# The first FFN half's router placed inside the last attention rows of an AdaLN attention and LoRA-MoE kernel, with a gate folded into the value weight

## What is computed

```python
mod = (silu(c) @ wmod)            # sa, ca, ga, sb, cb, gb for each batch; |ga|, |gb| at least 0.25
h = layernorm(x) * (1 + ca) + sa
x = x + ga * attn(h)              # attn: layernorm*gamma+beta, q k v, causal softmax, @ o_proj, + h
h = layernorm(x) * (1 + cb) + sb
x = x + gb * ffn(h)
# ffn:
gate_base, up_base = h @ Wg.T, h @ Wu.T
out = silu(gate_base) * up_base @ Wd.T
probs = softmax(h @ Wr.T); top-2 of 8 -> we for each expert
for each expert: hh = silu(gate_base + h@Ag.T@Bg.T*2) * (up_base + h@Au.T@Bu.T*2)
                 out += (hh @ Ad.T @ Bd.T * 2) * we
```

## Time and profile before

| | |
|---|---|
| time, median of 3 runs | 710.68 us (710.49 to 711.01) |
| profiled execution | 710.4 us, its span 708.6 us |
| granted TensorE clock, mean over the span | 0.992 |
| one batch | 165.9 us |
| PE busy | 665.5 us (94%), 3760 matmuls |
| PEld busy | 561.0 us (79%) |
| DVE busy | 509.1 us (72%), 1152 instructions |
| ACT busy | 340.2 us (48%), 604 |
| POOL busy | 392.2 us (55%), 518 |
| chain of work that ended last | PE 55%, DVE 28%, issue 9%, POOL 5%, ACT 2%, DMA 1% |

### The profile page before, as it was taken

One profiled execution on the slowest core, in us unless ns is written; L12 is line 12 of the kernel. 1 busy time (PEld: TensorE's weight loads), 2 busy tenths in 40 slices (PEclk: granted clock), 3 DMA queues, 4 the chain that ended last, 5 costly groups with the idle time before them and its releaser, 6 DMA issues.

```text
span 708.6 us, 10697 instructions
## 1 busy us (share of the span) xinstructions
PE 665.5 (94%) x3760; PEld 561.0 (79%) x3760; DVE 509.1 (72%) x1152; ACT 340.2 (48%) x604; POOL 392.2 (55%) x518
## 2 busy tenths in 40 slices
PE   5879999999999999999999999999999999999995
PEld 3669977877789987877788897887778997788884
DVE  5996786688976778578986678677988669536323
ACT  4534354535355345454355436364445535454542
POOL 3794457537772257456774238554775245743644
PEclk9989999999999999999999999999999999999999
DMA  8400010000000010000000002000000000000000
GB/s 303 117 1 1 1 61 1 0 1 31 0 2 31 1 61 1 0 1 31 0 1 31 1 1 61 0 1 1 30 2 1 31 1 1 0 1 1 31 0 31
DMA packets 14037, 15.44 MB, mean 22 GB/s; under 512 B 1312, under 2 KB 12704, under 8 KB 13984
## 3 DMA queue, kind: packets, MB, share of 16 engines
q1 hardware_dynamic: 13984, 14.76, 6.4%
HBM read 10.57 MB, written 4.19 MB: 21 GB/s over the span
## 4 chain that ended last, share of the span: by engine, by line
PE 55%; DVE 28%; issue 9%; POOL 5%; ACT 2%; DMA 1%; POOLq 0%; SPq 0%; DVEq 0%; ACTq 0%
PE ps L1198 50%; PE ps L1207 5%; DVE hid L1068 4%; DVE zb L799 3%; DVE zb L817 3%; POOL ring_lo L441 2%; DVE zb L804 2%; DVE stat L814 1%; DVE tm_hi L1058 1%; DVE tm_lo L1058 1%; DVE xr L817 1%; DMA xs<-in_L_attn_x 1%; DVE onehot L1019 1%; DVE stat L951 1%; DVE mv L791 1%
## 5 line engine op out<-in xcount | busy, mean ns | idle before, releaser
L441 POOL TENSOR_TENSOR ring_lo<-hid,ring_hi 128x512 fp32r<-128x512 f32 x144 | 192.3, 1342 | 104.2 <-ACT ring_hi L684 103.4
L676 ACT ACTIVATE act_s<-ps 128x512 f32<-128x512 f32 x120 | 71.8, 599 | 150.3 <-PE ps L1198 150.3
L1068 DVE TENSOR_TENSOR hid<-act_s,ps 128x512 f32<-128x512 f32 x120 | 81.5, 681 | 78.7 <-ACT act_s L676 69.5
L684 ACT ACTIVATE ring_hi<-hid 128x512 fp32r<-128x512 f32 (+1 forms) x144 | 90.3, 627 | 18.9 <-DVE hid L1068 10.2
L429 POOL TENSOR_TENSOR xr<-xr,xs 128x256 f32<-128x256 f32 x32 | 23.4, 733 | 91.8 <-DVE xr L959 91.8
L1198 PE MATMUL ps<-wdT_hi,ring_hi 128*128 128x256 f32 x192 | 53.1, 282 | 0.0
L1198 PE MATMUL ps<-wdT_lo,ring_hi 128*128 128x256 f32 x192 | 52.5, 279 | 0.0
L1198 PE MATMUL ps<-xT_hi,wgT_hi 128*128 128x512 f32 x96 | 39.3, 409 | 8.1 <-DVE hid L1068 8.1
L631 ACT ACTIVATE pT_hi<-ps 128x512 fp32r<-128x512 f32 (+3 forms) x48 | 21.8, 488 | 47.8 <-PE ps L1207 47.5
L1198 PE MATMUL ps<-wdT_hi,ring_lo 128*128 128x256 f32 x160 | 44.6, 279 | 0.0
L1198 PE MATMUL ps<-tm_hi,bgT_hi 128*128 128x512 f32 x96 | 40.6, 423 | 3.4 <-DVE hid L1068 3.3
(11 more groups left out here) (219 smaller groups left out, 2074.6 us busy)
## 6 DMA issues: line engine op xcount, KB each, us to landing
xs<-in_L_attn_x SPq DMA_DIRECT2D x4, 1024.0 KB, 5.6
out<-xr SPq DMA_DIRECT2D x7, 512.0 KB, 2.9
s_mod<-in_L_wmod SPq DMA_DIRECT2D x1, 1024.0 KB, 8.8
s_qkvT<-in_L_attn_qkv SPq DMA_DIRECT2D x1, 768.0 KB, 10.5
s_wg<-in_L_ffn_Wg SPq DMA_DIRECT2D x1, 704.0 KB, 8.0
s_wu<-in_L_ffn_Wu SPq DMA_DIRECT2D x1, 704.0 KB, 9.4
s_wd<-in_L_ffn_Wd SPq DMA_DIRECT2D x1, 640.0 KB, 8.3
s_mod<-in_L_wmod SPq DMA_DIRECT2D x1, 512.0 KB, 6.8
```

The costliest lines, as they stand in the source:

```text
L441: pool.tensor_sub(ring[1][:, place(n), :], hid[:, n % HID, :], ring[0][:, place(n), :].bitcast(fp32)).then_inc(h_lo.sem, 1)
L676: nc.scalar.activation(act_s[:, n % 2, :], ps[:, 2 * (n % 2), :], ACT.Silu).then_inc(silu_ready.sem, 1)
L684: nc.scalar.activation(ring[0][p0:P, place(n), :], hid[p0:P, n % HID, :], ACT.Copy).then_inc(h_hi.sem, 1)
L1068: V.tensor_mul(hid[:, n % HID, :], act_s[:, n % 2, :], ps[:, 2 * (n % 2) + 1, :]).then_inc(h_ready.sem, 1)
```

## The change

Its parts, as the code has them:

1. The gate GA of the attention goes into the value weight. `wvo` stays in fp32 as `wvo_full`; for each batch GpSimd multiplies it by the gate (`values_weight`), ScalarE makes the high part and GpSimd the low part. `x1_product` then adds `xs` itself and waits for `r_ready`; `x1_row` and the signal `x1_scaled` are gone.
2. The gated h is no longer made on VectorE. `residual` is a multiplication and an addition on GpSimd; rows 0 and 1 stand at r = 15 and 16 of the second half, rows 2 to 7 at the start of the next batch.
3. The second layer norm's `normalise` goes to ScalarE, as an activation with scale 1/sqrt and a bias `shift`, which costs one more small operation on VectorE (`neg_mean`) and one on GpSimd behind the Newton steps.
4. The first half's transposes, scaling and high parts move from step 8 into step 7 of attention, ahead of the last row's exponential on ScalarE; `probs_values(6)` moves behind the loop and holds `logits(0)`; the masks' transposes stand inside `probs_values(7)`.
5. In the first FFN half the Newton steps of rows 4 to 7 stand in one block at r = 2, the second group of transposes stands two units later, `logits(1)` in group 2, `router_probs(1)` and its followers one unit later, and `FILL` is a table for each half and group.
6. The next batch's first layer norm is cut into single steps (`ln1_centre`, `ln1_rows`, `ln1_stats`) for groups of rows, with two Newton blocks of 12 operations (`LN1_HA` at r = 10, `LN1_HB` at r = 16) in place of one of rows 0 to 7 at r = 13 and 14. The normalised rows 0 to 3 go to `tr_full`, rows 4 to 7 to `xr`.

```diff
@@ Signals, GpSimd @@
-        LN2_A, LN2_B, LN1_X, LN1_H = range(4)
+        LN2_A, LN2_B, LN1_X, LN1_HA, LN1_HB = range(5)
...
-        MASK_BANKS = ((7, 6, 4, 5), (3, 4, 5, 6))
+        MASK_BANKS = ((3, 2, 4, 5), (3, 4, 5, 6))
...
+                elif shifted:
+                    link(last)
+                    pool.tensor_mul(shift[:, lo:lo + n], neg_mean[:, lo:lo + n], y).then_inc(done, 1)
...
             def residual(b, i):
 
-                pool.wait_ge(t_gated.sem, t_gated.at(b, i))
+                link(pool.tensor_mul(gated[:, i % 2, :], zb[:, i, :], bc[:, b, GA, :]))
                 pool.tensor_add(xs[:, i, :], xs[:, i, :], gated[:, i % 2, :]).then_inc(r_ready.sem, 1)
 
-            def x1_row(b, i):
...
+            def values_weight(b):
+
+                pool.tensor_mul(gated[:, :, :], wvo_full[:, :, :], bc[:, b, GA, :].unsqueeze(1).to_broadcast([P, KT, D])).then_inc(wvo_scaled.sem, 1)
+
+            def values_weight_low(b):
+                pool.wait_ge(wvo_hi.sem, wvo_hi.at(b, 0))
+                pool.tensor_sub(wvo[1][:, :, :], gated[:, :, :], wvo[0][:, :, :].bitcast(fp32)).then_inc(wvo_lo.sem, 1)
...
-                for i in range(TC):
-                    x1_row(b, i)
+                for i in range(2, NT):
+                    residual(b, i)
...
                             if r == 2:
-                                newton(b, LN2_B, TC, TC, 0)
-                                newton(b, LN2_B, TC, TC, 1)
-                            if r == 3:
-                                newton(b, LN2_B, TC, TC, 2)
-                            if r == 7:
+                                for it in range(NEWTON):
+                                    newton(b, LN2_B, TC, TC, it)
+                            if r == 9:
...
-                            if 5 <= r < 5 + NT:
-                                residual(b + 1, r - 5)
-                            if r == 13:
-                                newton(b, LN1_H, 0, NT, 0)
-                                newton(b, LN1_H, 0, NT, 1)
...
+                            if r == 3:
+                                values_weight(b + 1)
+                            if r == 4:
+                                values_weight_low(b + 1)
+                            if r == 10:
+                                for it in range(NEWTON):
+                                    newton(b, LN1_HA, 0, TC, it)
+                            if r == 16:
+                                for it in range(NEWTON):
+                                    newton(b, LN1_HB, TC, TC, it)
...
+                            if r in (15, 16):
+                                residual(b + 1, r - 15)
@@ ScalarE @@
+            def normalise(i, dst, src, sig):
+                nc.scalar.activation(dst, src, ACT.Identity, bias=shift[:, i:i + 1], scale=rstd[:, i:i + 1]).then_inc(sig.sem, 1)
...
+                    if i == NT - 1:
+                        for k in range(KT):
+                            tr_high(b, KT * NC + k, xT[0][:, 0, k, :])
                     scores_exp(i)
...
+                    if i == NT - 2:
+                        act.wait_ge(rstd_ready.sem, rstd_ready.at(b, LN2_A))
+                        for tile in range(TC):
+                            normalise(tile, zb[:, tile, :], xr[:, tile, :], z2_ready)
@@ VectorE @@
-                    V.scalar_tensor_tensor(xr[:, t, :], ps[:, 6 + t % 2, 0:D], rinv[:, t:t + 1], bc[:, b, GA, :],
-                                           ALU.mult, ALU.mult).then_inc(x1_scaled.sem, 1)
+                    V.scalar_tensor_tensor(xr[:, t, :], ps[:, 6 + t % 2, 0:D], rinv[:, t:t + 1], xs[:, t, :],
+                                           ALU.mult, ALU.add).then_inc(x1_ready.sem, 1)
...
                 router_shift(0)
+                x1_product(NT - 2)
                 x1_stats(TC)
-                x1_stats(TC + 1)
                 router_probs(0)
                 router_top()
                 router_picks()
                 spread_masks(0)
-                x1_product(NT - 1)
-                x1_stats(TC + 2)
                 for g in range(2):
                     adapter_input_low(0, g)
+                x1_stats(TC + 1)
+                x1_stats(TC + 2)
+                x1_product(NT - 1)
...
-                        if 4 <= r < 4 + NT:
-                            ln1_h(b + 1, (r - 4,))
-                        if r == 4 + NT:
-                            moments(range(NT))
-                            guess(0, NT).then_inc(norm_ready.sem, 1)
+                        settle()
+                        for i in {4: (0,), 5: (1,), 6: (2,), 7: (3,), 10: (4, 5), 12: (6, 7)}.get(r, ()):
+                            ln1_centre(b + 1, i)
+                        for i in {5: (0,), 6: (1,), 7: (2,), 8: (3,), 11: (4, 5), 13: (6, 7)}.get(r, ()):
+                            ln1_rows(b + 1, i)
+                        for i in {8: (0, 1, 2), 9: (3,), 12: (4, 5), 14: (6, 7)}.get(r, ()):
+                            ln1_stats(i)
...
+                if not last:
+                    dve.wait_ge(rstd_ready.sem, rstd_ready.at(b, LN1_HB))
+                    dve.wait_ge(stored, b * (16 * NC) + 32)
+                    for i in range(TC, NT):
+                        normalise(i, zb, z_ready, z_tile(i))
@@ TensorE @@
-                    else:
-
-                        for k in range(KT):
-                            pe.wait_ge(z2_ready.sem, z2_ready.at(b, TC - 1))
-                            pe.wait_ge(probs_ready.sem, probs_ready.at(b, NT - 2))
-                            transposes(b, KT * NC + k, k, k, range(TC))
...
-                    if i >= 2:
+                    if i == NT - 1:
+                        pe.wait_ge(z2_ready.sem, z2_ready.at(b, TC - 1))
+                        for k in range(KT):
+                            transposes(b, KT * NC + k, k, k, [zb[:, tile, :] for tile in range(TC)])
+                    if 2 <= i < NT:
                         probs_values(i - 2)
...
-                FILL = (1, 2, 1, 1)
+                FILL = {(0, 0): (0, 0, 0, 0), (0, 1): (0, 1, 1, 1), (0, 2): (2, 2, 2, 1),
+                        (1, 0): (0, 0, 0, 0), (1, 1): (1, 2, 1, 1), (1, 2): (1, 2, 1, 1)}
...
-                pe.wait_ge(probs_ready.sem, probs_ready.at(b, NT - 1))
+                probs_values(NT - 2, range(PV_FIRST))
+                logits(0)
+                probs_values(NT - 2, range(PV_FIRST, NT - 1))
+                pe.wait_ge(pt_lo.sem, pt_lo.at(b, NPT - 1))
+                adapter_inputs(0)
                 probs_values(NT - 1, range(PV_FIRST))
-                logits(0)
+                pe.wait_ge(shifted_ready.sem, shifted_ready.at(b, 0))
+                pe.wait_ge(masks_spread.sem, masks_spread.at(b, 0))
+                for m in range(2):
+                    mask(0, m)
                 probs_values(NT - 1, range(PV_FIRST, NT))
-                adapter_inputs(0)
-                base(0, 0, 0, (0,))
```

More of the change, by code:

```diff
@@ L1230, in _, with transposes, attention_transposes @@
                 last_mm.then_inc(product_ready, 1)
-            def transposes(b, q, bank, k, tiles, src=zb):
-                for t, i in enumerate(tiles):
-                    last = transpose(ps[:, bank, t * P:(t + 1) * P], src[:, i, k * P:(k + 1) * P], ident[:, :])
+            def transposes(b, q, bank, k, rows):
+                for t, row in enumerate(rows):
+                    last = transpose(ps[:, bank, t * P:(t + 1) * P], row[:, k * P:(k + 1) * P], ident[:, :])
                 last.then_inc(transposed.sem, 1)
-            def attention_transposes(b, n, src=zb):
+            def attention_transposes(b, n, rows):
                 for k in range(KT):
@@ L1240, in attention_transposes @@
                     pe.wait_ge(z_ready.sem, z_ready.at(b, (n + 1) * TC - 1))
[L1241 removed]
+                    transposes(b, q, q, k, rows)
             def queries(b, js=range(4)):
```

223 lines of the change are left out of this document (115 added, 108 removed).

## The result

The changed kernel takes 725.59 us (median of 4 runs, 725.49 to 727.61) against 710.68: slower by 2.15% (ratio 1.0215, 95% interval 1.0198 to 1.0231). The forecast was 718.3; 725.59 lies just outside its range of 707.0 to 725.5. The direction was right, the size half of what came.

The account below looks back on a forecast made before the run. TensorE, busy 94%, could win only waits, which VectorE's and GpSimd's queues decide. First half 3.8 + between halves 0.6 + second half with tail 2.7 + setup 0.5 = +7.6 us: 718.3 for the median, range 707.0 to 725.5 (chance 0.8).

Parts of the forecast that it names:

- The first half: Attention with router and first FFN half: new waits sum to 3.15 against 2.19 before, +0.95 a batch, +3.8 for four.
- The wait of 0.6 at the first adapter: First FFN half: TensorE ready at 265.55, VectorE's hidden unit 0 at 266.1; new wait 0.6, where 0.98 was.
- The breaks listed for the kernel before: TensorE's issue breaks in the second batch, from 0.98 at the first adapter to 0.32 at 367.6: some 7.5 us.
- Between the halves: Between the FFN halves: hidden unit 17 comes 0.2 later against TensorE's arrival, +0.6 for three; bounds -0.9 and +1.5 a batch.
- Setup: Before the first batch: the values wait for the scaled weight, ready at 48.9 to 50.0; +0.5 (0 to 1.2).
- The gain of the second half: Second FFN half: row work in single steps removes breaks 1.48, 1.36 and 0.37; with the last 0.32, 3.53 a batch.
- The tail: End of second half: GpSimd 4.3 us later, 3.9 us of idle TensorE; net +0.9 a batch, +2.7 for three.
- the GpSimd queue behind unit 14: End of second half: the one slowing mechanism, deciding once its added steps exceed 1.8 + 3.5 us; Newton done at 371.4.
- the four normalisations: Tail: VectorE can start the last four only at 371.4 and needs 2.0 to 2.7 us for them.
- the clock: Rival, chance 0.30: half clock after the tail's idle time costs +2.1 a batch, 720.4 to 724.6 for one to three tails.
- the idle stretch at 700 in the earlier trace: Last idle stretch before the change: granted clock 1.00 at 700 to 701, TensorE back at 701.73; disagrees with the skill's rule.
- the rule of the Trainium skill in the prediction: Tail: such waits throttle TensorE each time around; by that all three tails would be slow, 724.6.

Follow-up runs that it names:

- Experiments 7: Changed kernel with layer norm in blocks, residual rows 0 and 1 at the next batch's start, and the last attention row's exponential ahead of both xT_hi copies: 699.85 us.
- 8: Kernel of Experiments 7 with VectorE's product of row 6 and statistics of row 4 moved behind the spread of the masks: 697.73 us.
- e1_fill: Changed kernel with 19 more matmuls of 512 columns in TensorE's idle time before the wait for normalised rows 4 to 7: 721.22 us.
- e4_blocks: Changed kernel with part 6 undone (next batch's first layer norm in blocks, one Newton block), the rest kept: 710.07 us.
- e8_before_residual_pool: Kernel before with only the gated product taken off VectorE; GpSimd makes the residual at the next batch's start, normalised rows go to other buffers: 715.34 us.
- e11_newton_later: Kernel of Experiments 7 with rows 4 to 7's moments and guess one unit later, Newton block at r = 4, ScalarE's normalisations at r = 7 and 8: 705.68 us.
- e3_newton_one: Changed kernel with one Newton iteration instead of three for rows 4 to 7 of the next batch's first layer norm: 717.03 us.
- e7_newton_split: Changed kernel with blocks and residual rows 0 and 1 at next batch's start, plus rows 4 to 7's Newton steps split over r = 3 to 5: 705.58 us.

## Why the forecast fell short, point by point

- **The first half held.** Forecast: four waits of 1.15, 0.7, 0.6 and 0.7, +0.95 a batch. Measured: 0.97, 0.65, 0.52 and 0.77; from the scores to the inputs of the second half +1.06. Experiments 7 and 8 take two of them out, each by the cause that the step named. The wait of 0.6 at the first adapter came as 0.52, but its terms do not give it: 257.65 with 1.27, 0.75, 0.5, 4.1 to 4.7 and 0.69 is 265.0 to 265.6, not 266.1. What makes up for it is a wait of VectorE itself, for which there was no term:

```profile
266.67 0.48 DVE L992 SCALAR_TENSOR_TENSOR xr<-ps,rinv,xs 128x256 f32<-128x256 f32 x1 [0.83 <-PE ps L1240]
```

The breaks listed for the kernel before add up to 7.0 a batch, not 7.5; the forecast does not use that sum.
- **Between the halves held:** +0.1 a batch for 0.2 (bounds -0.9 and +1.5).
- **Setup came near its size, 0.9 for 0.5, by another cause.** The scaled weight was to make the values wait. In the profile of the changed kernel they do not wait (49.98, right behind the queries): the queries start 0.75 later, behind the transposes of the first rows, and run at half clock for longer. In e1_fill, with the same setup, the queries start 0.65 later and the values do wait 0.36 for the weight, the clock is back earlier, and the first scores start at 51.98, where 51.96 was.
- **The gain of the second half held in size:** 3.70 for the forecast 3.2 without the last wait. Its cause was given as the single steps, and that is wrong. With blocks (e4_blocks) it stays at 37.75; with the gated product alone taken away (e8_before_residual_pool) it is there too.
- **The tail is the step that failed,** "slower by one mechanism: the GpSimd queue behind unit 14". The mechanism was right: the Newton block ended where the sum said. (The net of this step, 4.3 less 3.53, is 0.8 a batch; +0.9 was written.) Two sizes were not right. First, the four normalisations, "2.0 to 2.7", took 4.06, and those of rows 2 and 3 made TensorE wait another 1.1, which had no term. The rows were there: in the kernel before, the same operation took 0.40 us with GpSimd idle and 1.36 to 1.39 beside its low parts, as in this place of the second batch:

```profile
274.32 2.67 DVE L817 TENSOR_SCALAR zb<-xr,mv,rstd 128x256 f32<-128x256 f32 x2 [0.23 <-POOL rstd L408]
...
274.24 3.89 POOL L441 TENSOR_TENSOR ring_lo<-hid,ring_hi 128x512 fp32r<-128x512 f32 x3
```

The forecast's 0.5 to 0.68 a row lies between the two, for a place where GpSimd's queue would be full. Without the clock the tail gives +5.7 a batch (13.55 in e1_fill less 7.85), where 4.3 was forecast.
- **Second, the clock.** It had been put as a rival at 2.1 a tail, chance 0.30, and came true with 2.1 in the second tail. Tails and clock: forecast 718.3, plus 1.4 x 3 for the tail, is 722.5 (e1_fill, where only the clock is mended: 721.2), plus 4.4 for the clock by e1_fill is 726 to 727, measured 725.6. The forecast let a wait of 3.9 us pass at full clock on the ground of one row, the idle stretch at 700 in the earlier trace rows. That stretch was 2.96 us long; the one of 3.98 in the setup, as long as the wait forecast, had the clock at 0.50 behind it:

```profile
39.96 1.94 PE L1207 MATMUL ps<-ident,xr 128*128 128x128 f32 x8 [3.98 <-DVE xr L817]
...
701.73 0.38 PE L1198 MATMUL ps<-bdT_hi,tm_hi 128*128 128x256 f32 x1 [2.96 <-DVE tm_lo L1081]
```

And the last stretch is no safe ground either. It is 2.96 us long in every run; the clock stays at 1.00 through it in the kernel before, but in e11_newton_later TensorE comes back from it, at 696.67, to half clock:

```profile
696.00:697.00 1.00, 0.33 (x1) 0.33 (x2) 0.62 (x1) 0.00 (x0) 0.00 (x0) 0.50 0.00 0
```

Every tail of the changed kernel's profile has the clock at 0.50, for 5.6, 4.7 and 3.4 us of work. That each such wait throttles the engine anew, as the rule of the Trainium skill in the prediction has it (TensorE: Matmul & The Clock Gate, section HAM oscillation), agrees with these three tails.
- **The chances.** Each of the two misses alone stays within 707.0 to 725.5; both together leave it by 0.1 us. The range took the clock with the forecast's tail, and the longer tail without the clock, though the longer wait is what makes the low clock likelier: they should have been one case.

Still open: why a wait of 2.48 costs the clock in two tails of e3_newton_one and not in the third, and what made the profiled run of the changed kernel 2 us longer than the other three. Its first scores stand 0.9 later than in e1_fill, which has the same setup, and its tails differ by up to 1.0, both with the time at half clock; but the others have no trace.

## What to carry to other kernels

Row work that is spread between the units of a pipelined loop must be finished before the loop's end: what stands last in the queues meets the next stage's first need, and a late start of one small block stops everything. Cost an operation of VectorE beside GpSimd at its row in such company, not at a mean; and where a new wait of 2.5 us or more on TensorE is forecast (the shortest here that cost the clock), take its clock into the same case, not into another. Here a change of six parts that lost 15 us held a gain: without part 6 and with the two residual rows at the start of the batch it is worth 6.6 us, and with two reorderings 13. The gain is that of the second half, 3.5 a batch in three batches, from the gated product off VectorE. The router inside attention lost 1.0 a batch as it stood, was even after the first reordering and won 0.7 after the second. Parts 1, 3 and 5 were not taken away one by one.

## What was not expected of the hardware

- A VectorE operation on 128 by 4 elements took 1.27 us beside a GpSimd operation of 1.27 us, and 0.16 to 0.17 without (e7_newton_split; 0.88 and 1.14 in e11_newton_later): a small operation can take as long as the one beside it.
- After a wait of 1.5 or 1.7 us and some 2.5 us of work, the granted clock fell in or 1 us behind a wait of 2.5 us (two of three tails of e3_newton_one); it stayed up in the third tail, and in e4_blocks with waits of 1.26 and 0.83.
- One stretch of 2.96 us without TensorE work, the same in every kernel, passed at full clock in one trace (before) and ended at half clock in another (e11_newton_later).
- Nineteen matmuls that compute nothing made the kernel 4.4 us faster, by holding the clock at 2.4 GHz through a wait of 4.7 us.
